# ScalarE writes the score mask ahead of the copy of the attention outputs' high part

## The reference, cut to what matters

```python
s1 = where(allowed, q1 @ k1.T * scale, NEG)      # allowed: j <= i and j > i - 64
s2 = where(allowed, q2 @ k2.T * scale, NEG)
diff = relu(softmax(s1) - lam * softmax(s2))
diff = diff / (sum(diff) + 1e-6)
out = (diff @ v) @ Wo
```

## Time and profile before

| | us |
|---|---|
| median of the runs | 1347.83 |
| span of the profiled execution | 1343.3 |
| TensorE busy | 1269.2 (94%) |
| VectorE busy | 843.1 (63%) |
| ScalarE busy | 715.6 (53%) |
| GpSimd busy | 470.9 (35%) |

### The profile page before, as it was taken

The page is one execution under the profiler, slowest core; times in us unless marked ns, Lnnn a source line. Parts: engine busy times, 40 slices in busy tenths (PEclk is TensorE's granted clock), DMA queues, the critical chain, the costliest instruction groups (busy, mean ns, idle before and its releaser), DMA issues.

```text
span 1343.3 us, 27486 instructions
## 1 busy us (share of the span) xinstructions
PE 1269.2 (94%) x9712; PEld 989.2 (74%) x9712; DVE 843.1 (63%) x1986; ACT 715.6 (53%) x2746; POOL 470.9 (35%) x467
## 2 busy tenths in 40 slices
PE   5799999999999788999999999989899999999998
PEld 4578888888887565666666666557788888888887
DVE  6788888888888676666656656765453333433333
ACT  2788888889887553444444444465232332423322
POOL 3122113112212134544544534541053353533532
PEclk9999999999999899999999999999999999999999
DMA  6011001100102101002002001000325342254230
GB/s 221 16 25 49 18 17 25 49 17 17 31 19 92 35 1 76 1 1 76 1 1 75 1 1 60 1 1 1 107 58 142 74 120 56 39 137 78 56 93 31
DMA packets 29810, 64.54 MB, mean 48 GB/s; under 512 B 6912, under 2 KB 12160, under 8 KB 28416
## 3 DMA queue, kind: packets, MB, share of 16 engines
q1 hardware_dynamic: 29696, 63.05, 17.6%
HBM read 52.42 MB, written 2.23 MB: 41 GB/s over the span
## 4 chain that ended last, share of the span: by engine, by line
PE 74%; DVE 10%; ACT 7%; issue 4%; POOL 2%; DMA 2%; SPq 1%; DVEq 0%; POOLq 0%; ACTq 0%
PE ps L531 31%; PE ps L923 9%; PE ps L647 5%; PE ps L716 4%; PE ps L679 4%; PE ps L820 4%; ACT ea L1434 3%; PE ps L810 3%; PE ps L792 3%; PE ps L800 2%; PE ps L670 2%; PE ps L586 2%; DMA cw<-comb_d 2%; ACT ea L1478 1%; DVE xnt L991 1%
## 5 line engine op out<-in xcount | busy, mean ns | idle before, releaser
L1798 POOL TENSOR_TENSOR sg<-sg,cw 128x512 f32<-128x512 f32 x88 | 113.5, 1290 | 260.1 <-ACT sg L1597 253.1
L1375 DVE TENSOR_TENSOR hh<-ps,sg 128x512 f32<-128x512 f32 x100 | 69.2, 692 | 178.6 <-POOL sg L1798 162.0
L1401 ACT ACTIVATE hhh<-hh 128x512 fp32r<-128x512 f32 x100 | 63.2, 632 | 214.7 <-DVE hh L1375 214.7
L1401 ACT ACTIVATE pt<-ps 128x512 f32<-128x512 f32 x128 | 76.9, 600 | 179.3 <-PE ps L800 122.6
L1434 ACT ACTIVATE ea<-ps,negmax 128x64 f32<-128x64 f32 (+1 forms) x512 | 164.6, 341 | 6.0 <-DVE negmax L1127 6.0
L531 PE MATMUL ps<-xnh,wch 128*128 128x512 f32 x400 | 157.0, 393 | 0.7 <-ACT pt L1401 0.7
L1174 DVE TENSOR_TENSOR qcs<-ps,tabb 128x512 f32<-128x512 f32 x192 | 123.6, 686 | 53.4 <-PE ps L531 53.1
L531 PE MATMUL ps<-xnl,wch 128*128 128x512 f32 x400 | 156.9, 392 | 0.0
L531 PE MATMUL ps<-xnh,wcl 128*128 128x512 f32 x400 | 155.6, 389 | 0.0
L1665 POOL TENSOR_TENSOR ea<-ea,rden 128x128 f32<-128x128 f32 (+1 forms) x128 | 62.1, 506 | 256.2 <-DVE rden L1083 256.2
L1672 POOL TENSOR_TENSOR eb<-eb,rsum 128x512 f32<-128x512 f32 x64 | 66.9, 1045 | 160.3 <-DVE rsum L1218 160.3
(11 more groups left out here) (153 smaller groups left out, 3349.6 us busy)
## 6 DMA issues: line engine op xcount, KB each, us to landing
raw_w<-in_rawb_dram SPq DMA_DIRECT2D x4, 2432.0 KB, 9.0
kva<-ktmp SPq DMA_DIRECT2D x64, 128.0 KB, 2.4
cw<-comb_d SPq DMA_DIRECT2D x32, 256.0 KB, 5.0
raw_w<-in_rawc_dram SPq DMA_DIRECT2D x4, 1920.0 KB, 8.0
cw<-comb_d SPq DMA_DIRECT2D x16, 224.0 KB, 4.3
raw_a<-in_wqk_dram SPq DMA_DIRECT2D x4, 768.0 KB, 5.4
cw<-comb_d SPq DMA_DIRECT2D x16, 192.0 KB, 6.0
cw<-comb_d SPq DMA_DIRECT2D x16, 160.0 KB, 5.5
```

The source lines that it names most:

```text
L1375: dve.tensor_tensor(hh[:, par, :], bank(C_U[par]), sg[:, par, :], ALU.mult).then_inc(c_h, 1)
L1401: return act.activation(dst, src, ACT.Copy)
L1798: pool.tensor_tensor(sg[:, par, :], sg[:, par, :], cw[:, c % 2, t, :], ALU.mult).then_inc(c_hs, 1)
```

## The change

ScalarE's copy of the mask, with its wait for the exponentials of its own unit, moves in front of the copy `oah` with its two waits. Both are in every unit that has both; nothing else is touched.

```diff
                 slot(1)
+                if not drain and not (final and u >= UN - 2):
+                    act.wait_ge(a_ex, n + 1)
+                    copy(A_S[u % 2][:, :, 0:SW], maskb[:, :].unsqueeze(1).broadcast_to([128, 2, SW])).then_inc(a_mk, 1)
                 if two:
                     act.wait_ge(a_pv, n - 1)
                     wait(act, a_wo, n - 3)
                     copy(by_head(oah[:, (u - 2) % 2, :, :]), by_block(bank(OB))).then_inc(a_o, 1)
-                if not drain and not (final and u >= UN - 2):
-                    act.wait_ge(a_ex, n + 1)
-                    copy(A_S[u % 2][:, :, 0:SW], maskb[:, :].unsqueeze(1).broadcast_to([128, 2, SW])).then_inc(a_mk, 1)
```

## The result

The changed kernel takes 1368.69 us (median of 4 runs, 1366.79 to 1369.03) against 1347.39 us (four runs of the kernel before: the three behind its 1347.83, and one of 1345.82): a ratio of 1.0156, 95% interval 1.0141 to 1.0170, 21.3 us more. The forecast was 1370.9. The profiled execution spans 1365.0 us, 21.7 more than the one before (1343.3), where the sum said 1366.4.

A forecast was written before the change was run, and what follows sets the result against it. The prediction took the loop of ScalarE and VectorE, with 1.06 us of room a chunk, to bound the changed kernel. Chunks +18.9 and units outside 3.7 and 0.5 made +23.1: span 1366.4, median 1370.9, range 1359 to 1378.

The forecast's parts named there:

- the sum: Twelve first-attention chunks 338.2 against 319.4 us, +18.9; units outside add 3.7 and 0.5; together +23.1, span 1366.4.
- point 1: On ScalarE, the mask ahead waits for its unit's exponentials, starting at +2.71 instead of +2.53: 0.18 us standing still.
- point 2: On ScalarE, the mask holds the next copy 0.74 us: `oah` starts at +3.45, 0.92 later; copies behind only 0.18 later.
- point 3: VectorE's `oal`, and what follows it, waits for `oah`: the unit becomes 6.82 us against 5.90.
- point 4: At j = 0 to 1, `oah` ends near +4.07 and `oal` starts at +4.85 anyway: the delay costs nothing.
- point 5: The score matmuls read the mask two units on, with 5.3 us of cover: the earlier mask brings nothing.
- The step from span to median: Whole kernel: the median of the runs lies 4.5 us above the profiled span, turning 1366.4 into 1370.9.
- Rival A: First attention: TensorE, 99% busy, hides the delay; time stays 1347.8 us; chance 6%.
- Rival B: Each chunk pays 0.92 us once, where VectorE's k take feeds TensorE's chain; 1363.0 us; chance 14%.
- the loop without TensorE: ScalarE and VectorE's loop in a regular chunk: 7.56 + 3 × 6.82 = 28.02 us, longer than TensorE's 26.32.
- Rival C: The earlier mask lets scores start earlier, by up to 0.29 us a unit; 1343.4 us; chance 2%.
- rival D: Idle TensorE gets less clock, about 1383 us at 0.90, or a new wait for `oal`; from 1377 up, chance 10%.

The follow-up runs named there:

- e6: Kernel before, with an unused copy of the mask's size ahead of `oah` in all units that have a mask, mask still behind: 1370.98 us, ratio 1.0178.
- e1: Kernel before, with the mask moved ahead of `oah` only in units j = 0 (first of a chunk's four): 1347.48 us, ratio 1.0004.
- e10: Kernel before, with e9's change and the mask of units j = 2 moved into the next unit, behind the value copy: 1342.69 us, ratio 0.9971.
- e2: Kernel before, with the mask moved ahead of `oah` only in units j = 1: 1357.27 us, ratio 1.0070.
- e5: Kernel before, with the mask moved ahead of `oah` only in units j = 1 and j = 3: 1367.66 us, ratio 1.0154.
- e7: Changed kernel, with an unused copy of the mask's size added between the mask and `oah`: 1402.65 us, ratio 1.0410 to the kernel before.
- e8: Kernel before, order unchanged, with an unused copy of the mask's size added behind the mask: 1358.96 us, ratio 1.0079.
- e9: Kernel before, with ScalarE's `wah` copy of the second slot put behind `oah` in chunks with weight copies: 1344.40 us, ratio 0.9987.

## Why the prediction was right, point by point

- *The mask's wait* (point 1): forecast 0.18, in the trace +2.69 in place of 2.53, 0.16. Right, slightly over.
- *The copy behind it* (point 2): 0.74 forecast, 388.03 to 388.78 is 0.75. Right. `oah` was 0.91 late, forecast 0.92.
- *The unit* (point 3): 6.82 forecast, 6.77 measured. The 0.05 is in the step from `oah` to `oal`, 0.61 in place of 0.66, since the copy took 0.58 in place of 0.62. Why it was shorter is open: in e6 it also runs wholly behind the exponentials and takes 0.62.
- *Cover at j = 0* (point 4): shown by e1, 26.31.
- *Nothing from the earlier mask* (point 5): no run gained from it, and e10 gains by a later one.
- *The sum*: twelve chunks 17.2, forecast 18.9. The three chunks with weight copies took 85.1 (forecast 85.1), the six regular ones 167.6 (168.1), and the three with `woh` 83.8 (85.0), so most of the 1.7 lies there: 28.01 in the one shown, where 28.33 was forecast. The reading behind that term was wrong. The forecast took the slow unit, 6.95, as bound by ScalarE's queue and added 0.18; in the kernel before, `pt` starts in it at +5.40, 0.04 after TensorE's transposes have ended, as in rows 6, though the copy ahead of it lets it start at about +5.17. After the change the queue does bind it, `pt` starts at +5.34, and the unit takes 6.88. The opening (units 2 to 8) gave 2.9 and units 56 to 61 1.6; forecast 4.2 for both, measured 4.5, of which some 0.6 is the clock (last section). That these pieces add up to the 21.7 of the spans is chance: the first exponential came at 32.05 in place of 33.05, though nothing ahead of it had changed (31.84 to 33.51 in the twelve traces), and units 61 and 62 took 0.6 longer.
- *The step from span to median*: the forecast added 4.5, measured 3.7 (1368.69 less 1365.0). Each run's time is 1.8 above its span; the rest is how far the profiled execution lies below the median, and it is not a constant. So of the 2.2 us between 1370.9 and 1368.69, 1.4 is in the span and 0.8 in this step.
- *Rival A* falls: TensorE is busy 95% of the chunks now, was 99%, and its 99% hid 0.30 of the delay at j = 1 and nothing at j = 3. The Trainium skill's rule of the most contended engine (Perfetto Trace Analysis, Identifying the Most-Contended Engine), read as the prediction reads it, would have mispriced the edit by all 21 us. The section itself judges TensorE's headroom not by its matmuls but by its weight loads, among others; these were busy 263.75 of 319.37 us, 83%, and ScalarE 86%, so it does not name TensorE as plainly as the prediction says.
- *Rival B* was mispriced, and the reason given against it was only half of the truth. "The room is 1.06 us a chunk" treats the slack at j = 2 as free for TensorE. e2 shows that it is not: TensorE's chain has a second door, the take of q2 ahead of the v projection, with 0.30 us to spare. Priced with both doors TensorE's loop is 27.88, not 27.24, and it ties with the loop that I had summed. That the second loop, which I had not summed, came out no longer than the first is luck: had it been longer, the forecast would have been too low. That only the loop without TensorE bounds the new kernel, as the forecast said, is refuted by e5.
- *Rival C* falls by the 5.3 us of cover, *rival D* by the granted clock of 1.00 over 336.57 us with 16 us of idle TensorE in pieces. Its price had a slip: 26.4 us of work at 0.95 and 0.90 of the clock are 27.8 and 29.3, not 27.7 and 29.0; nothing of the forecast rests on it. A new wait of TensorE did come, but it was inside the price.

## What to carry to other kernels

Before an in-order engine's instructions are exchanged, look for each of the two at the row of its reader: one that starts 0.04 to 0.06 us after its end, as here, has no room, one that starts 5 us later has plenty, and the second goes behind. Sum every loop that the delayed one is in, and for a loop through the busiest engine count each place where it takes something over from the others, also those where no wait shows today: the gap between the end of the one and the start of the other, less the 0.05 of the hand-over, is all the room there is. An engine that is not the busiest can hold the time, as ScalarE does in e7 (25.88 us busy of a chunk of 30.11): what matters is the length of its loop, not its share.

## What the runs showed of the hardware that I had not expected

The granted clock can drop after one short wait, and does so in some executions only. Near unit 57 TensorE stands 2.16 to 2.18 us for GpSimd in every trace. In five of the twelve (the kernel after, e1, e5, e6, e8) the clock then falls to its lower level, 1.2 GHz, shortly after TensorE has started again; in the other seven it stays at 2.4. These are ten microseconds around it in the kernel before, in e1 and in the kernel after:

```profile
417.00:427.00 10.00, 7.83 (x83) 6.36 (x83) 8.52 (x30) 6.00 (x31) 4.15 (x6) 1.00 0.50 139
```

```profile
417.00:427.00 10.00, 7.84 (x60) 5.89 (x60) 7.12 (x25) 6.16 (x29) 4.16 (x6) 0.83 0.57 160
```

```profile
436.00:446.00 10.00, 7.83 (x57) 5.74 (x56) 7.89 (x27) 6.10 (x30) 4.05 (x6) 0.83 0.49 131
```

Within them, two microseconds of the kernel after:

```profile
443.07:445.07 2.00, 2.00 (x4) 0.86 (x4) 1.54 (x4) 2.00 (x15) 0.00 (x0) 0.50 1.02 240
```

With 0.83 the next unit takes 7.33 us (e1) or 7.35 (after), with 1.00 it takes 5.91 in the kernel before. In e1 this unit has the same instructions in the same order as before, so there the 1.4 us are the clock's alone. What decides between the two was not tested. The profiled execution after has this drop, so some 0.6 us of its 1.6 at the end is not the change's (in e2, where the same `oah` is late and the clock stays up, the unit takes 6.79).

A small operation of VectorE stretches while GpSimd works. In the kernel before, in a chunk with weight copies:

```profile
105.06 1.46 POOL L1653 TENSOR_TENSOR wal<-raw_a,wah 128x256 fp32r<-128x256 f32 x2
...
105.86 0.68 DVE L1066 TENSOR_TENSOR rho<-ratio,a_gap 128x4 f32<-128x4 f32 x1
```

`rho` on 128 x 4 elements takes 0.68 us and ends with GpSimd's split of the weight tile at 106.5; it takes 0.16 elsewhere. In e9 the split ran in two pieces, one that ended 0.7 earlier and one that ended 0.5 later (counted from the unit's first exponential), `rho` was back at 0.17, and the four differences, which now ran beside the second piece, took 1.29 in place of 1.00. That the two engines hold each other up is the reading that fits both; no run here tested it alone.
